# Another step order for a two-flow perceiver kernel on one core, without its constant matmul products

## What is computed

```python
x = x + _L0_xattn_ref(_layernorm(x, axis=-1), ctx_768, ...)
x = x + _L0_attn_ref(_layernorm(x, axis=-1), ...)
x = x + _L0_ffn_ref(_layernorm(x, axis=-1), ...)
x = x + _L1_xattn_ref(ctx_768, _layernorm(x, axis=-1), mask_BxS2_bk0, ...)
x = x + _L1_attn_ref(_layernorm(x, axis=-1), ...)
x = x + _L1_ffn_ref(_layernorm(x, axis=-1), ...)
x = x + _L2_xattn_ref(_layernorm(x, axis=-1), ctx_768, ...)
x = x + _L2_attn_ref(_layernorm(x, axis=-1), ...)
x = x + _L2_ffn_ref(_layernorm(x, axis=-1), ...)
x = x + _L3_xattn_ref(_layernorm(x, axis=-1), ctx_768, ...)
x = x + _L3_attn_ref(_layernorm(x, axis=-1), ...)
x = x + _L3_ffn_ref(_layernorm(x, axis=-1), ...)
return x
```

## Time and profile before

| what | value |
|---|---|
| median of 3 runs | 2556.38 us (2555.1 to 2557.56) |
| span of the profiled execution | 2557.4 us |
| TensorE busy | 2254.9 us, 88% |
| VectorE busy | 1746.6 us, 68% |
| ScalarE busy | 1368.6 us, 54% |
| GpSimd busy | 774.0 us, 30% |
| mean granted TensorE clock | 0.971 of 2.4 GHz |

### The profile page before, as it was taken

The page is one execution under the profiler, slowest core; times in us unless marked ns, Lnnn a source line. Parts: engine busy times, 40 slices in busy tenths (PEclk is TensorE's granted clock), DMA queues, the critical chain, the costliest instruction groups (busy, mean ns, idle before and its releaser), DMA issues.

```text
span 2557.4 us, 62072 instructions
## 1 busy us (share of the span) xinstructions
PE 2254.9 (88%) x26420; PEld 1506.9 (59%) x26556; DVE 1746.6 (68%) x4832; ACT 1368.6 (54%) x2287; POOL 774.0 (30%) x676
## 2 busy tenths in 40 slices
PE   5889999877988888998888888888988889999999
PEld 3556666655565554565655666665656556555666
DVE  5775666577667777676777778777767674556642
ACT  4667676545555665545666544344455544555542
POOL 3323446432342212122222122211223223323443
PEclk9999999989999999999999999999999989999999
DMA  3011313100000000010000000000000102121132
GB/s 115 19 41 34 80 45 75 42 24 9 9 11 14 8 8 6 1 47 10 17 16 10 19 25 25 25 16 17 10 11 16 58 8 71 40 55 54 55 104 62
DMA packets 50452, 84.14 MB, mean 33 GB/s; under 512 B 9536, under 2 KB 24768, under 8 KB 49792
## 3 DMA queue, kind: packets, MB, share of 16 engines
q1 hardware_dynamic: 50176, 80.18, 11.3%
HBM read 77.54 MB, written 2.62 MB: 31 GB/s over the span
## 4 chain that ended last, share of the span: by engine, by line
PE 57%; DVE 25%; ACT 8%; issue 4%; POOL 3%; DMA 1%; SPq 1%; another core or an unknown queue 0%; DVEq 0%; POOLq 0%; ACTq 0%
PE psum L946 6%; PE psum L908 5%; PE psum L904 5%; PE psum L1606 3%; PE psum L463 2%; DVE c_L3x_most L1726 2%; PE psum L1699 2%; DVE c_L2x_mx L2081 2%; PE psum L1984 2%; DVE c_L2x_p L2087 1%; PE psum L471 1%; PE psum L1395 1%; PE psum L1976 1%; PE psum L773 1%; PE psum L778 1%
## 5 line engine op out<-in xcount | busy, mean ns | idle before, releaser
L893 POOL TENSOR_TENSOR c_L3f_h<-c_L3f_h,c_L3f_spread 128x512 f32<-128x512 f32 x96 | 121.3, 1283 | 188.8 <-DMA c_L3f_spread<-scratch 103.1
L471 PE MATMUL psum<-halves_held 128*128 128x512 bf16 x454 | 131.0, 403 | 14.0 <-issue 9.8
L936 DVE TENSOR_TENSOR c_L3f_h<-c_L3f_h,psum 128x512 f32<-128x512 f32 (+1 forms) x112 | 75.9, 682 | 76.5 <-PE psum L908 52.0
L922 ACT ACTIVATE c_L3f_h<-psum 128x512 f32<-128x512 f32 (+1 forms) x112 | 65.5, 594 | 110.2 <-PE psum L904 99.1
L946 PEld LDWEIGHTS psum<-weights,c_L3f_h 128*128 128x128 f32 (+1 forms) x896 | 108.1, 193 | 19.3 <-issue 15.3
L946 PE MATMUL psum<-weights,c_L3f_h 128*128 128x128 f32 (+1 forms) x896 | 112.9, 279 | 0.0
L904 PE MATMUL psum<-c_L3f_xT,weights 128*128 128x512 f32 x208 | 107.4, 601 | 0.0
L908 PE MATMUL psum<-c_L3f_xT,weights 128*128 128x512 f32 x208 | 107.4, 603 | 0.0
L471 PEld LDWEIGHTS psum<-halves_held 128*128 128x128 bf16 x588 | 54.3, 102 | 74.8 <-issue 35.1
L893 POOL TENSOR_TENSOR c_L0f_h<-c_L0f_h,c_L0f_spread 128x512 f32<-128x512 f32 x64 | 82.5, 1313 | 50.4 <-DVE c_L0f_h L936 39.2
L1606 PE MATMUL psum<-c_L3x_qx,c_L3x_kT 32*128 32x256 f32 x512 | 77.1, 427 | 21.1 <-DVE c_L3x_most L1726 17.4
(11 more groups left out here) (640 smaller groups left out, 6520.0 us busy)
## 6 DMA issues: line engine op xcount, KB each, us to landing
c_L0f_spread<-scratch SPq DMA_DIRECT2D x64, 256.0 KB, 5.5
c_L3f_spread<-scratch SPq DMA_DIRECT2D x32, 512.0 KB, 5.3
c_L2f_spread<-scratch SPq DMA_DIRECT2D x64, 128.0 KB, 3.1
c_L3f_spread<-scratch SPq DMA_DIRECT2D x64, 128.0 KB, 5.8
c_L0x_ctxT<-ctxT SPq DMA_DIRECT2D x8, 384.0 KB, 7.8
c_L1x_ctx<-ctx SPq DMA_DIRECT2D x16, 192.0 KB, 2.4
c_L2x_ctxT<-ctxT SPq DMA_DIRECT2D x8, 384.0 KB, 3.6
c_L3x_ctxT<-ctxT SPq DMA_DIRECT2D x8, 384.0 KB, 3.7
```

Source lines behind the costliest of these rows:

```text
L471: nc.tensor.matmul(j.psum[:, bank, :], j.half["ident"], j.half["take"], start=True, stop=True)
L893: nc.gpsimd.tensor_tensor(h, h, j.m["spread"][:, f, :], ALU.mult).then_inc(*j.up("mixed"))
L922: nc.scalar.activation(j.m["h"][P - rows:P, f, :], j.psum[0:rows, 1 + 2 * f % 3, 0:j.tok], ACT.Silu).then_inc(*j.up("silu"))
```

## The change

One string is replaced, and nothing else: `ORDER` holds the same 8114 letters and nine `+` in another order, and none of its 198 digits (their sum was 588). With no digit `warm` is always 0, and `pe_warm` issues nothing. `PLAN`, the programs, the tiles and the places in SBUF and PSUM are as before. The new order was found by a replay of the trace. The diff, cut to the first, some middle and the last lines of the string:

```diff
--- before
+++ after
@@ -2838,76 +2838,74 @@
 
 ORDER = (
-    "vqQDDddDVdldkdddp8paglPLaDKQqDpDDLPaApgApGp7PvvdDavAkGKvvpPPP1paVVa3pgdAdaVpgdVlVPp1pA2PGvQvA4PDadvAkPGPlPvdvkV1pVa3pDDA"
-    "dLdvvDavvadavlVKpVvVPPAApGQPvvvA1PlvGvPvvdPDgkdVv9pVgAaVVVPpApGpapaDpaDLapDKQppvvpPaApDvavvaPavDkdpddDLA1PvlGpPvDvKvPvVV"
-    "vAvvVgldVvVP5PAG1pAQDPapDAGPPaPpVDVLpgAVaaVDVPppakppKDpDDdvLvp1PaApDAGvva4PavavApkGPvPdpdPvvvVdvlVvAKVvvVgVLv+P1pVgAPaVD"
...
-    "PrrvrrrrarrdVPrprAvPrkVGkPpAcpa1PabVspAvvsNpZspaMZZpQavYWggcvgWcgcWGcXcNvDpdYMdNXYMaNX1MZZNWWDMZ1pZZaWpYWWpavXNvpdvlY3Mv"
-    "lgvNXgaMY1NXMWZW2MDZvNgWpLWWppZXp2MZdZYpvXNvMYvX3MaNWWvMYpWNaZWZ2NWaXZpZZMvYppv1NvXvvvpYMvDvNvXMYKNW1pWZZPvA2PgvVPvDgvPA"
-    "vDVGPpAapPrVpAprprdbrNrrrrZaapkrrMvkrZprvprarZpcapbvY8NsDWLsWWsXpgYMgNXgcGYcNMZZvNagXvMZccWcZWZvpMaYpWWdpWavXp1NvaMYddvl"
-    "pXldvgMNXvMYaNWDgWkZMZvKpgW1NWWpZXppZZp3MvYdvXNvaMvYpXNMYkWNWMZaZ4NaWWWpZXp5MZZvYvpvvXNvvpYvMvXvNpYMvNWZgWZPvvAgPvvpVa+V"
...
-    "prRRRPRaACcBVPASDvpVPSPASpVPPAapVvpaGbPsLPAGPVDpvGsPaGApsVPGvPAsGPVPASgCVgCsPPASPVPApVCCpPpAGaPvGPVpAgaPKgPVvPGACVgPpGCa"
-    "GACVgCCGCgCgCCCVSPpApPaPRvPRRgBRRpRRpRARvCgPBaSpApvSVPgPVSpAaPSvPVgPASGPVPAGPVGPAPGVPAGPVPGAPVGPAGPVPAGPVPGApVpGapvPaPvA"
-    "PVPGAPVcAVcccccccccccccCvsCCCCCCCCCCCCCVS")
+    "dDqDddldkqQdddplVDpaaLDKQDdDDvPgpaPAgApLpkGpvPvDaAGvvVvpaPPKgPpaVpAdagVdVdVPApplpvPlAvaPGdAQDGPkPvPdvvDkVDpLVadAdDdvlvav"
+    "dpavvaKpVVvVPPAApvvGkPvAlvGPvQvvdPgPVvpVgADDaDLVVaVPpDpapapapAppKDDDLDQpvvpPaAapaPaKpAPkdvvdvvdlGGvdldpvvPvPvVVAvvvgVVvV"
+    "PAkPApgDDaPGApQGpaPPkPVpVDpALaaaVDVVPppAppKvGDvpPaAvavpvaPvDaDAdLdLpGPvdDPlpvKvdPvVvVAvVvVvVVgPvApg+aVAVPVApVDApkPpapaaP"
...
+    "rrdrrPdavVrrPAPcpPQAbVPpAVaavGpsvGNMZpZappkZasvggWsWccggWcvYcDcDDvNXYMNpXYMNXZZaMWWNMpakdZZZaWWppWYpvNvXvgYMvLNvXvadMYdX"
+    "NlMWWZZgMgpWWpWNppZZXpZMvYvDXNvMaXvMWYWpMNYWWNZaZaWNpZZXZdMvpvYpvvXNvvpvYMvXNvYMWNWZpZvPgAvlvPgKVDPvDDdAvPPpaApVrPrrpAbp"
+    "pVrGrrrarrNvrkaMZpkrrZprrcbpZavpWpWvsWYNXYsMgNgsXpYcNGZMZgaavXNvgccMLZWcWZcZDvpaMWpWdYWpavddplNXalvdvdYMgpXNMXvYMvNWkWvk"
+    "ZgZMagNWWKppWppZZpXZMvYvXNvMavYXpNMYWWNZaZMaWWpNWpZZXZMvvvYvpvXvvNvMvYpXNYpMNvZWZWgvvPAgvvPpaVPDpDrArVprbrrrrVrAVrPrrprA"
...
+    "GApVpVapGPGPPVpvarprPDrArppbPRPvRaRRAPRrrPBRPDDrrpvRarpAVpVcaPAPbVPRRvpvPPCBpAapvpVaPSAspvpVPAPVPAPVpPAsPaVPAPSVPGAPSGVC"
+    "GCSGpGpsPGACGSCgCGsCLPgVPsvAGPVPGDAPgCKgCagvCGpaGpvPgVACgVCCCCVSPApapPRRBRPRRRPRRAPAVcPVpPAPaVPRAPVPvAPCPApBvPVcVPASPVPA"
+    "PVpcPAPaVPASPVcGcSGpGCSGPAGPSVGPAcGcGPgVPgAPgVCvgCCGCgPGAcGpGaCvcccccCcvCVCCsCCCCVS")
```

More of the change, by code:

```diff
@@ new lines @@
+    "pKDVVVVpaVDpVVpvVvGpaVDpGbPLApLDrrprrrrPrrrADPrrrAPrrAPdrAPrrrrPrKPPaVvVPcAbpdaVAVPsAVpVApvdplKDPapaVpvsvPVgVspVagpsVpgV"
+    "aVscgVDcGcVDcPvApgvpLPLDAPAPGPKPAAPPPVDVPAppaaPAcApAckPcKDDdDVLVgVVvvggLVcvPVpVaVDVpbVpVVpaGppVvPGdrAprarrDPdrrrPrArrPAr"
+    "rArPdrrArPrvPrrKrPPaVVPcbpAvpasAPApAppaPpsapsPKDDVVDVLVlDvLvVgVgVpsVgpKVsagcVVcgDVdvcGcVcPGApagpPAPAPAPAPPkPPVVPAcvvgVAV"
+    "PgVAcVAcvpadPpbppaPpappKDVrrrrrrvdrVrrVrVrrvrprarpvrarpVpvrrarpVpVVcvbDpGapVapvDPvdsAplpGPALPDdAPAPAPksPPgsKPgsVcgaVcsqg"
@@ new lines @@
+    "DcDPgvAdcgdcgPBgRdcRRlcddRRcRRRRPvRAPRRRPRpkRaPVRApRRapqvRVpRdddPCAldBadDapgPaVPSkvgAPvLvvPVAPVPdAgPdVPvAPSvPVppGASpaaGP"
+    "SaVGCDSCGpGCvGvCGCavlCvGKdCdCVPApavPDBDpRRaDRRPRLpRRkvpaPvpdRRRDadpdRRlpRRRARqaRRRapgRPaVCvBgPAvdvPVAPkVPSdAgPvPpvpdadpa"
+    "ValPAVpPvvddS+PPaGvSGvCASGApavGPSVGkpaGPpvppaVdavpGapagAqpPaVCgvKCvGvdCCCgdCvlCvppaVdpaPdaddAklpPvvPaPvPvBRdRpRavRRRApDR"
+    "aRRRpRvpkdPdaDpdDdRRapRldARavpRaVqRgRRRpVCvaPBddgPkAvvPVAPSVPAgPvLPpvDpdapVaaPAVpPvSvPGSPavGCSvlCAASGpavGCVGdpaCGpvpkGva"
@@ new lines @@
+    "PddpddapVapagqvGplCaCgKCvvdCdVPADdgPDBvRPRvPpRARdRaPVpRpRaRRaRRRkRARpRPvRvRPRRRPaVDCvBLPvldpAavVSpkaPApVvppaddaddpapagSl"
+    "pGdSqPadAvPgvPvGAvCSVdPSVCgdPvGPpvpapGaaPlAAGpGCvvDCVdaCvGkCvkpavPdpaCpvppadddapVvpKGaaqgpCaVPAgvlvPvdBdRPdPAQgPvpvdpRaR"
+    "paldaDdDkVApPvvRPVPavPvApaAvRPDRRLRRpkRaRVpVRRRDvppaapRRRaRpvRKgaRDpvCaPBAgPvPvAVPSPAgvpvpapadVaDDddplSPvdPGvSPVGSaCvGCv"
+    "SkGpaGvCLpGaGpvvCApddaCVDDpGpKvCvCvdCvVgDPAgppPvPvQvaAApGPAgvPvDppAVaVGVpVlVdDapaGpLVvvVvvpPPAAPAvDKvppDapaPapVDpDVkLvvA"
@@ new lines @@
+    "vvDVVpvpaPVKpApvPAvPvvpVPgPpVAvgPvvaAApGPAvvPdddpDQ+pADDaGDVplaLDpDaDdVVpkvvGvvVpPPAvvpVpDaPALAgDpaPpaVDVpvAvvvVVpvpaPKV"
+    "pKpAvPvApvPvVPPAgDDvPpgvvQdDaVdALApGPAvdvVPDDppADaGVpVapaGpvvvvVpPPAAvvpVpDaPLAgplaPpaVdVpvkvvvAVVpvpaPAVppvpvPpAvDPvKgd"
+    "VPKVgAvPvPdvDaDQDDAdApLPGAvPvDppADDaGVVpVapaGVpDLvVvgvlvpPPAAPAvvppapaPapVVdpAvvvvVkDKVDpKvAPpVadvvvvpaavPvvAvvvPvVPvPvA"
+    "vvvAvvPdvvdAvvPpDDlaVDvQALPpGvdAvGVVpVDaDDKpapGVVDkpPvALpPPAvgAagpapvPpVgvVppgAVDpVpvvVvpaPAvvKpvaadPvvAvvvPdvvdvDvvvvVP"
@@ new lines @@
+    "PAAPvvvAvvPDpDAGVaVlDvdvPpQLvDADGvVpVDapapGvVkpVgDpPPAvPaAgApLaDpKvPpVKgvVppgAVpVpvvVvpaPAvvpvaadPvvAvvvvPvvvvvvVPPAAvPv"
+    "vDvAvdPpDDaVdvvAlPQpGvdAvGVVpVapapGVDVLpDPPADPADDpAvKvPgVagpVapLvpAVpgVDDkpvPAVpgKPApPVPAVvvDDGVvpPaAPAPAPDdAvvvpGaaVVvv"
+    "vdvvvvvvGvvvdvvvvlVpLVPvavPvAApvPvApaPVDVppAVaVpvdKPAVgpvkapgPaApvpPVVgpvppgP+ApqvPvPPPVVVvVGVGDpVVqvappAavPvpgagnVVPPAz"
+    "DDzPzAmPwwyddAwndlyPLnVyGVnVzVzxPmxVnDmVxmzwzwzmwPwPyAwnPxymnxymnxzzmwAwnAPPzKmVzVVVwPzwVPAwPyPVPVnxVyVmGnDxVmGxymVwnwzz"
@@ new lines @@
+    "VmAwwnPwPzzxzmyVxVnyPmxnPymwnAwzzdDDpaLDPApvApPaPkddvdqpplVVKaPvVpVagVGnVPPAzzmzPAwwPwynxAmyPxnyVnVzmzxVVnmzwzPwzdwwwVPA"
+    "mPyPnPPyVnVxyVVmnVGzzxGnmGxzmVVzwAzwPymVnwwynwynVzzPPDxDDmLxngAmxzzmwwPzAmAPwwPwyVDVnVxVyPmnxVymnxzzmwwPkpVaPApvdpddPaAq"
+    "pApPaPvpvagVVlKmVnwVwwPzzzdVPAPxPPPVmyVxVnVmyGDxnVmDywGwnzzVnVAzmwzPwzwyVnxVyPPAmxPmxnmywwnzAzmAnwwPkPwzzDxLzgVmVVyGVPxn"
+    "myVxnmyVDwwPPnzAzmPwwAnPwAPzzKVzxVVVmyxPVnPDVDymAnxymw+nwzVzVVPpAaAVVVVpVVVvVVVpVVVDVVaVpPAPpavVVpvVagVLVDnmzzKPzAwwPdPy"
```

94 lines of the change are left out of this document (34 added, 60 removed).

## The result

The changed kernel takes **2643.1 us** (median; 2638.1 to 2648.0), the kernel before in the same comparison 2555.8. The ratio is **1.034 (95% interval 1.0325 to 1.0355)**: 87 us slower. The forecast was 2535 us and the other sign, and 2643 lies outside the range of 2485 to 2595.

What follows compares the result with a forecast made beforehand. No engine alone bounds it: two flows alternate on TensorE (88% busy), which waits when both are on VectorE or ScalarE. Terms -29 + 29 - 22 + 1 = -21 us gave 2535 us against the 2556.4 median; range 2485 to 2595.

Steps and rivals of the forecast that it cites:

- Part 1: TensorE, line 471: removing 588 constant products frees the time of those standing before real work; -29 us, bounds 0 and 131.
- Part 2: TensorE's clock, mostly 500 to 2110 us: without products, 110 us more at half clock, 0.26 us each; +29 us.
- rival B: 500 to 2110 us: unfilled waits let the clock fall, 300 us more at half clock; 2584 us, chance 0.26.
- Part 3: All engines' queues: the new order covers more of TensorE's trips through other engines; -22 us, ends -30 and +22.
- The late L2f load: SyncE's queue: L2f's weights are issued behind one more transfer, a context load of flow 1; +1 us, range 0 to 4.
- turning point: Added half-clock time at which the forecast sum changes sign: 192 us, mean clock near 0.93, from 50/0.26.
- C: Gain and clock cancel: the waits are VectorE's and ScalarE's, a covered trip makes the next late; 2556 us, chance 0.12.
- D: VectorE's queue blocks: the new order loses 22 us instead of winning them; 2579 us, chance 0.08.
- E: Ahead of 2110 us, trips hanging on several queues shorten together, closing a quarter of TensorE's rest; 2484 us, chance 0.12.

Runs made afterwards that it cites:

- 32 late bursts: Kernel before without 32 bursts (99 products) that ended after their step's operands were there and had no half-clock stretch beside them: ratio 1.0028, +7 us.
- the late products only: Kernel before, old order, keeping only the 61 bursts (224 products) that ended after their step's operands were there: ratio 1.0197, +50 us.
- the two mixed runs: Against the kernel before, products kept: TensorE's queue new, others old, ratio 1.0369 (+94 us); TensorE's queue old, others new, 1.0378 (+97 us).

## Why the prediction was wrong, point by point

**Part 1, the products' gain: -29 us forecast, 0 to 3 us by the runs.** The failed step is the choice within the bounds. The prediction named the right mechanism for its lower bound ("0, if another wait is always late next") and then took the chain's share of line 471 as if all of it came back. Leaving out 32 late bursts freed 16.0 us at the next step and 0.6 us three steps later. A share of the chain is what was last in that run, and not what comes back without it; nor is it a sure price of *adding*, for which the 29 us gave the right number (+19 measured, +18 expected) while the chain's own share rose by some 40 us. The 131 us, which the prediction called rather low, are indeed low: 134 records are missing, and in the kernel with TensorE's queue new, where none is, the same 588 products take 177 us.

**Part 2, the price of the clock: 0.26 us for each us at half clock forecast, 0.27 measured.** The working stood, in the run that comes nearest to changing the clock alone (the late products only); in the changed kernel itself it is 0.30 (87/291; by the mean of its four executions 87/311 = 0.28), if all of its loss is put down to the clock, and 0.28 along before's own 49 executions.

**Part 2, the amount: 110 us forecast, 291 measured.** This is the step that turned the sign: the choice of 110 near the lower bound. The bounds were 39 and 320, the upper one from the stages' busy shares without line 471 (clock near 0.86 there), and the stages after show 0.82, 0.85, 0.94 and 0.87. The lower bound had TensorE's rest nearly right (382 us; 2646.7 - 2251.9 = 395 measured), but half-clock time did not grow in proportion to the rest: 440 us instead of 186. The prediction went toward the lower end because "inside the half-clock stretches the products were there too and had not held the clock". That looks only at the places where the products failed. Where they succeeded there is no half-clock stretch to be seen, and the trace of before cannot show it but through the busy share that would be left. The half-clock stretches that remained are a poor sample: even 253 further products did not remove them.

**The rule that spoke against the change.** The stretches at 0.82 and 0.87 are stages in which TensorE stops for other engines again and again. The Trainium skill, "TensorE: Matmul & The Clock Gate", in "HAM oscillation — how this bites in real kernels", describes the slow clock that such stops bring; the prediction cited it for its rival B, and the trace of the changed kernel agrees: 395 us in which TensorE does nothing instead of 302 (the products counted as work), and 59 half-clock stretches instead of 28.

**Part 3, the order: -22 us forecast, +17 with the products, about 0 without.** The prediction counted how much TensorE work the order puts under each trip through other engines, one trip at a time, and found 29 us more under cover. It kept +22 as an end, by mirroring. The run with the new order alone is within that end; the two mixed runs show why the count says little: the same queue of TensorE costs +94 us with the old queues of the others. What a trip meets in the queues of the other engines is not in the count, and it is as large as anything in it. The late L2f load, +1 us: no cost is seen. L2f's first step starts 11.4 us behind the load's issue (12.7 before); its weight loads stand idle for 0.8 us ahead of it, the matmuls not at all.

**The rivals.** B was the right one, mechanism and place, with chance 0.26. Its time, 2584, was too low because it kept the -50 us of parts 1 and 3: with 291 us, no gain and 0.27 it is 2556 + 79 = 2635, and with the mean of its four executions and the price along before's own, 311 x 0.28, it is 2643. That leaves nothing for the order. Its turning point, 192 us with a mean clock near 0.93, rested on the same 50 us; without them there is none, and each added us costs. C was wrong (nothing cancelled). D's sign for the order alone was right; its place, VectorE's queue, was not confirmed. E did not happen.

**What would show it.** Mean clock under 0.93 meant rival B: 0.917. Half-clock time was to be 257 us, and is 440; that nearly all of it lies between 500 and 2110 us of before's time holds: by the stage rows 118 + 96 + 67 + 126 = 407 us. TensorE's busy time was to fall by some 110 us: it fell by 3, since the added work at half speed was 254 us. The last stage within 5 us of 447: 450.8, right. The wait behind L2f's exponential slightly under 20.5 us: 24.4, wrong. Neither of the two other signs of a wrong forecast came: the clock did not stay at 0.97, and VectorE's waits on GpSimd did not grow by tens of us (the longest group 16.6 us before, 21.5 after).

## What to carry to other kernels

Price a filler by what would happen to the clock without it, from the busy share that real work alone leaves in each stage, and not from the places where the filler failed; here, in one case, that share gave 320 us for a measured 291. Read a wait that grows when a filler goes over real work alone, or the filler's own time is taken for new waiting. A share of the chain is no price: before a removal is booked as a gain, look up the next step's own wait. And look at the spread among executions of the unchanged kernel: here it gave the price of the clock, 0.28, without any experiment. An order in which several queues were laid out together is changed as a whole or not at all; a count of single trips covered did not even give its sign.

## What the runs showed of the hardware

588 small bf16 products on TensorE, in 198 bursts, kept 294 us of this program from running at 1.2 GHz and were worth 90 us (3.5%), though they put 131 us of recorded matmuls (177 us where all records are there) on the engine that the chain names first. The effect is graded: 0.4 to 0.5 us at half clock for each product left out where whole bursts go (294/588; 186/364 and 95/224 for the two kinds), 0.27 where each burst is halved (63/234). And it ends: from 588 to 841 products nothing more was gained. A us at half clock cost 0.27 us, not the half us that a matmul loses in it (in the trace of before, products one behind the other start every 216 ns at full clock and every 427 ns at half): TensorE is not always at work in it, and not always what the others wait for. The clock also differs between executions of the same kernel, 0.967 to 0.979 for before, and some 20 us of its span go with it.
